# Two transformer blocks on one core: projections ahead of the block boundary, parts loaded into 48 partitions, and expert results scattered to token order

## The reference

```
xn = layernorm(x)
s  = attention(xn)          # block 0: linear attention, 16 heads of 16; block 1: causal softmax attention with ALiBi, 16 heads of 16
g  = mixture(xn)            # router, the 2 best of E experts per token, plus one shared expert
x  = x + s * silu(g)

mixture: y = shared_mlp(xn) + sum over the 2 chosen experts of share_r * expert_r(xn)
         expert(x) = (silu(x Wg) * (x Wu)) Wd,  inner size 176;  E = 8 in block 0, 16 in block 1
         share = the two best router values, divided by their sum
```

## Time and profile before

| | |
|---|---|
| time, median of 3 runs | 731.95 us (731.43 to 732.06) |
| profiled execution: its own time, its span | 733.88 us, 732.1 us |
| mean granted TensorE clock | 0.937 |
| experts 0 | 134.1 to 225 us |
| shared 0 | 225 to 340.4 us |
| first scores of sequence 0 | 374.0 us |
| first transposed scores (attention proper) | 394.4 us |
| experts 1 | 587.3 to 669.9 us |
| shared 1, chunks 1 to 3 | 669.9 to 709.3 us |
| end of the span | 732.1 us |

### The profile page before, as it was taken

How to read it: one execution, slowest core, us unless ns; L and a number is a source line. 1 busy time by engine, 2 the same in 40 slices (tenths; PEclk the granted TensorE clock), 3 DMA queues, 4 the chain that set the end, 5 groups by cost and what they waited for, 6 DMA issues and landing times.

```text
span 732.1 us, 12664 instructions
## 1 busy us (share of the span) xinstructions
PE 612.6 (84%) x4090; PEld 483.0 (66%) x4090; DVE 410.4 (56%) x992; ACT 331.3 (45%) x715; POOL 158.1 (22%) x172
## 2 busy tenths in 40 slices
PE   2989993699999998999558899998988789999750
PEld 2958882599998887886344565666665468886430
DVE  6176664255544365656726756645543456665468
ACT  2223331366555444444513435444445468886331
POOL 0127533000004440401301013221122100002662
PEclk9999997699999999999859989999999989999985
DMA  9903553343322950201693854767922035542334
GB/s 323 310 29 125 146 161 130 91 130 116 117 83 83 277 114 8 59 0 41 133 127 100 120 111 110 150 97 160 173 60 66 1 96 163 160 153 87 90 101 134
DMA packets 85560, 86.64 MB, mean 118 GB/s; under 512 B 19727, under 2 KB 77026, under 8 KB 85218
## 3 DMA queue, kind: packets, MB, share of 16 engines
q1 hardware_dynamic: 78842, 68.92, 38.1%
q0 software_dynamic: 6144, 16.79, 7.8%
q10 hardware_dynamic: 512, 0.13, 0.1%
HBM read 51.40 MB, written 34.28 MB: 117 GB/s over the span
## 4 chain that ended last, share of the span: by engine, by line
PE 39%; DVE 8%; ACT 4%; DMA 2%; issue 2%; SPq 1%; POOL 0%; ACTq 0%; DVEq 0%
PE bank L821 5%; PE bank L885 4%; PE bank L909 3%; PE bank L1019 3%; PE bank L1045 3%; PE bank L972 3%; PE bank L1063 2%; PE bank L873 2%; PE bank L668 2%; PE bank L1021 2%; PE bank L1047 2%; PE bank L839 2%; PE bank L896 1%; DVE mneg L1915 1%; DMA KS<-projection_parts 1%
## 5 line engine op out<-in xcount | busy, mean ns | idle before, releaser
L589 POOL DMA_INDIRECT slots<-xn,slot_of x64 | 66.6, 1041 | 167.7 <-DMA slots<-xn,slot_of 100.4
L1915 DVE TENSOR_REDUCE mneg<-bank 128x2 f32<-128x512 f32 (+1 forms) x96 | 62.7, 685 | 51.0 <-PE bank L1021 50.4
L1752 DVE TENSOR_TENSOR xgl<-bank,xgh 128x256 f16<-128x256 f32 (+1 forms) x86 | 36.4, 424 | 51.9 <-ACT xgh L1310 51.9
L602 POOL DMA_INDIRECT rets<-results,slot_of x32 | 33.4, 1042 | 139.3 <-DMA results<-ys 97.6
L1726 DVE TENSOR_TENSOR hf<-bank,sg 128x512 f32<-128x512 f32 x36 | 24.7, 690 | 61.5 <-PE bank L821 56.8
L1019 PE MATMUL bank<-KS,QS 99*128 99x256 bf16 (+1 forms) x256 | 38.7, 261 | 20.4 <-DMA KS<-projection_parts 11.8
L602 POOL DMA_INDIRECT gu<-results,slot_of x32 | 31.4, 982 | 112.2 <-DMA results<-ys 96.5
L873 PE MATMUL bank<-cf,xn 128*128 128x128 f32 x172 | 36.3, 295 | 19.5 <-DMA xn<-slots 17.1
L1420 ACT ACTIVATE exps_first_keys<-bank 128x512 f32<-128x512 f32 x64 | 34.8, 597 | 29.4 <-PE bank L1047 29.4
L1285 ACT ACTIVATE sg<-bank 128x512 f32<-128x512 f32 x36 | 21.3, 599 | 56.1 <-PE bank L821 56.1
L1759 DVE TENSOR_TENSOR hs<-bank,gs 128x176 f32<-128x176 f32 x86 | 29.3, 341 | 28.9 <-ACT gs L1316 24.4
(11 more groups left out here) (221 smaller groups left out, 1609.6 us busy)
## 6 DMA issues: line engine op xcount, KB each, us to landing
xn<-slots SPq DMA_DIRECT2D x86, 128.0 KB, 2.2
results<-ys SPq DMA_DIRECT2D x86, 128.0 KB, 1.7
projection_parts<-parts SPq DMA_DIRECT2D x16, 384.0 KB, 2.8
QS<-projection_parts SPq DMA_DIRECT2D x48, 128.0 KB
KS<-projection_parts SPq DMA_DIRECT2D x48, 128.0 KB
slots<-zrow SPq DMA_DIRECT2D x1, 6016.0 KB, 21.9
x<-in_x SPq DMA_DIRECT2D x8, 512.0 KB, 6.0
x<-in_w SPq DMA_DIRECT2D x4, 704.0 KB, 8.2
```

Source lines behind the costliest of these rows:

```text
L589: pool.indirect_dma_start(out=slots_dram, out_offset=bass.IndirectOffsetOnAxis(ap=at, axis=0), in_=xn[:, t, :], in_offset=None).then_inc(s ...
L602: pool.indirect_dma_start(out=rets[L][:, t % RETS, r, :], out_offset=None, in_=results_dram[L], in_offset=bass.IndirectOffsetOnAxis(ap=at, ...
L1752: dve.tensor_tensor(xgl[L][:, j % 2, :], PS[j % 2][:, 0:D], high[:, j % 2, :], ALU.subtract)\
L1915: dve.tensor_reduce(mneg[:, qt, h0:h0 + heads], PS[6 + p % 2][:].rearrange("p (n k) -> p n k", n=heads), AX.X, ALU.max, negate=True).then_ ...
```

## The change

1. Six projections (j = 0 to 5) move into `shared(0)`, behind items 15 to 18, 21 and 22, all through PSUM bank 7, with their high and mid parts on ACT, rests on DVE and low parts on POOL. They share one `rest` buffer. The parts of chunk 0 are stored, and sequence 0 is loaded when 22 of 24 down products are done.
2. The DRAM layout of the parts has a fourth copy, so that three parts of a query or key lie side by side. A sequence is loaded by 4 DMAs of 48 partitions instead of 12 of 16. The heads take another order in memory (`column(h)`).
3. The 20 stores of slope and position rows move behind `expert_rows(0)` on SP's queue.
4. A new `first_scores` on PE interleaves sequence 0's scores with the front and router of chunks 2 and 3. DVE interleaves its maxima with the last combinations, updates and normalisations. The Exp of block 1's routing and the copy of the shared down weights on ACT come behind `attention(-1)`.
5. Block 1's row scatters wait for every fourth instead of each. Behind them POOL scatters, for each slot, a label of two numbers (8 bytes: the row of the result in token order, and the token's share). A table of labels is filled at the start with rows past the end, for slots without a token, and read back before experts 1 (`slot_labels`).
6. In experts 1, ACT multiplies each result tile by the share as it copies it (Identity with a scale), and POOL scatters it from `ys` straight to `results_by_token` (47 indirect DMAs) instead of SP's store. SP loads the results of one chunk with two direct DMAs of 512 KB, POOL adds the two experts of each token, and DVE adds the sum. The gather and DVE's `combine` of block 1 go.
7. `shared(1)` for chunks 1 to 3 is one run of nine items on ACT and DVE too, with the additions, silus and updates between the items; the x copies of chunk 2 move into experts 1, and PE's first shared gates stand before the wait for the last result.

```diff
-EARLY_BANK = (0, 1, 2, 3, 1, 2)
+EARLY_BANK = 7
+EARLY = {15: 0, 16: 1, 17: 2, 18: 3, 21: 4, 22: 5}
...
-    parts_dram = nc.dram_tensor("projection_parts", (NCH, 2, 3, 2, 2, P, SEQ), BF16, kind="Internal").ap()
+    parts_dram = nc.dram_tensor("projection_parts", (NCH, 2, 4, 2, HD, H, SEQ), BF16, kind="Internal").ap()
...
+    labels_dram = nc.dram_tensor("slot_labels", (SLOTS[1] * P, 2), F32, kind="Internal").ap()
+    returned_dram = nc.dram_tensor("results_by_token", (2 * NTOK * P + SLOTS[1] * P, D), F32, kind="Internal").ap()
...
+            sp.wait_ge(tokens_set, 2)
+            sp.dma_start(labels_dram.rearrange("(j p) c -> p j c", p=P), unused_labels).then_inc(labels_cleared, 16)
...
             expert_rows(0)
+            sp.wait_ge(rows_set, 3)
+            for h in range(H):
+                sp.dma_start(position_rows_dram[:, h, :], position_row[SLOPE_ROW:ALL_ROWS, :]).then_inc(rows_stored, 16)
+            for n in range(SEQ // 64):
+                sp.dma_start(slope_rows_dram[:, :, 64 * n:64 * n + 64], slope_row[SLOPE_ROW:MAX_ROW]).then_inc(rows_stored, 16)
...
+            def store_parts(i, kind):
+                sp.wait_ge(part_low, after(4 * i + kind + 3))
+                for copies, which in ((slice(kind ^ 1, 3 + (kind ^ 1)), slice(0, 3)),
+                                      (slice(3 * kind, 3 * kind + 1), slice(2 * kind, 2 * kind + 1))):
+                    sp.dma_start(parts_dram[i, kind, copies].rearrange("t b d (h a) n -> (d h) t b (a n)", a=2),
+                                 parts[:, kind, which].rearrange("p t b a n -> p t b (a n)"))\
+                      .then_inc(part_stored[kind], 16)
...
-                for kind, (dst, order) in enumerate(((QS, Q_PART), (KS, K_PART))):
-                    for place, part in enumerate(order):
-                        sp.dma_start(dst[slot][HD * place:HD * place + HD].rearrange("d (a h) n -> d a (h n)", a=2),
-                                     parts_dram[i, kind, part, b].rearrange("a (d h) n -> d a (h n)", d=HD))\
+                for kind, dst in enumerate((QS, KS)):
+                    for u in range(2):
+                        first = 1 - u if kind else u
+                        sp.dma_start(dst[slot][3 * HD * u:3 * HD * (u + 1)].rearrange("p h n -> p (h n)"),
+                                     parts_dram[i, kind, first:first + 3, b].rearrange("t d h n -> d t (h n)"))\
...
+            store_parts(0, 0)
+            store_parts(0, 1)
+            sp.wait_ge(s_down, SHARED[0] * NCH - 2)
+            load_rows(0)
+            load_sequence(0)
...
+            sp.wait_ge(labels_sent, 16 * 2 * NTOK)
+            sp.dma_start(slot_labels, labels_dram.rearrange("(j p) c -> p j c", p=P)).then_inc(labels_landed, 16)
             expert_rows(1)
+            for n in range(YRING):
+                sp.wait_ge(returned[n], 16 * len(range(n, SLOTS[1], YRING)))
+            for c in range(NCH):
+                if c >= 2:
+                    sp.wait_ge(combined, NTOK + 2 * (c - 1))
+                for r in range(2):
+                    row = r * NTOK * P + c * CH
+                    sp.dma_start(rets[1][:, TPC * (c % 2):TPC * (c % 2) + TPC, r, :],
+                                 returned_dram[row:row + CH, :].rearrange("(t p) d -> p t d", p=P))\
+                      .then_inc(back_landed[c % 2], 16)
...
+            low_parts(range(6))
...
+            scatter(1, 4)
+            pool.wait_ge(scattered[1], 16 * 2 * NTOK)
+            pool.wait_ge(ex_set, once(1, 1))
+            pool.iota(own_labels[:, :, 0], [[P, 2 * NTOK]], base=0, channel_multiplier=1,
+                      allow_small_or_imprecise_dtypes=True).then_inc(tokens_set, 1)
+            pool.wait_ge(tokens_set, 3)
+            pool.wait_ge(shares_set, 1)
+            pool.wait_ge(labels_cleared, 16)
+            for n in range(2 * NTOK):
+                if n and n % 8 == 0:
+                    pool.wait_ge(labels_sent, 16 * n)
+                pool.indirect_dma_start(out=labels_dram,
+                                        out_offset=bass.IndirectOffsetOnAxis(ap=slot_of[:, n:n + 1], axis=0),
+                                        in_=own_labels[:, n, :], in_offset=None).then_inc(labels_sent, 16)
...
+            pool.wait_ge(returns_set, 1)
+            for j in range(SLOTS[1]):
+                pool.wait_ge(ey_sb, tile(1, j + 1))
+                pool.indirect_dma_start(out=returned_dram,
+                                        out_offset=bass.IndirectOffsetOnAxis(ap=returns_to[:, j:j + 1], axis=0),
+                                        in_=ys1[:, j % YRING, :], in_offset=None).then_inc(returned[j % YRING], 16)
+            for n in range(NTOK // 2):
+                c, at = n // 2, 2 * n % RETS
+                pool.wait_ge(back_landed[c % 2], 32 * (c // 2 + 1))
+                pool.tensor_tensor(rets1[:, at:at + 2, 0, :], rets1[:, at:at + 2, 0, :], rets1[:, at:at + 2, 1, :], ALU.add)\
+                    .then_inc(pair_summed, 1)
...
+            def next_front(k):
+
+                c, n = k // SHARED[0] - 2, k % SHARED[0]
+                j = EARLY.get(k)
+                if j is not None:
+                    if j == 0:
+                        pe.wait_ge(s_a1, 16 * (4 + HD))
+                        pe.wait_ge(columns_set, 16)
+                    pe.wait_ge(xt_sb, half(1, 2 * (j // 4) + 2))
+                    pe.wait_ge(part_rest, after(j))
+                    project(j, EARLY_BANK)
...
+            def first_scores():
+
+                scores(0, 0)
+                scores(0, 1)
+                value_bias()
+                front(1, NCH - 2)
+                for p in (2, 3, 4):
+                    scores(0, p)
+                router(1, NCH - 2)
+                for p in range(5, 11):
+                    scores(0, p)
+                front(1, NCH - 1)
+                scores(0, 11)
+                max_transposes(0)
+                pe.wait_ge(vbias_ready, 1)
+                pe.wait_ge(s_sb[1], after(0))
+                values(0)
+                pe.wait_ge(lg_read, NCH - 1)
+                router(1, NCH - 1)
+                j = projected(-1)
+                pe.wait_ge(v_sb, after(1))
+                project(j, PROJECT_BANK[0])
+                project(j + 1, PROJECT_BANK[1])
...
+            pe.wait_ge(eh_set, tile(1, SLOTS[1]))
+            shared_gates(1, SHARED[1])
             pe.wait_ge(ey_sb, tile(1, SLOTS[1]))
-            shared(1, (1, 2, 3), nothing)
+            shared(1, (1, 2, 3), nothing, begun=True)
...
+                        if j >= YRING:
+                            act.wait_ge(returned[j % YRING], 16 * (j // YRING))
+                        act.activation(ys1[:, j % YRING, :], PS[6 + j % 2][:, 0:D], ACT.Identity,
+                                       scale=slot_labels[:, j, 1:2]).then_inc(ey_sb, 1)
...
+            def rest_part(j, bank):
+
+                bias = 2 * (j % 2) + j % 4 // 2
+                dve.wait_ge(part_high, after(j + 1))
+                dve.wait_ge(part_low, after(j if j < 6 else j - 1))
+                dve.scalar_tensor_tensor(out=by_sequence(rest_of(j)), in0=by_sequence(PS[bank][:]),
+                                         scalar=c1_heads[:, bias:bias + 1], in1=part_of(j, 0),
+                                         op0=ALU.add, op1=ALU.subtract).then_inc(part_rest, 1)
...
+            def add_returned(n):
+
+                at = 2 * n % RETS
+                dve.wait_ge(s_res, half(1, n + 1))
+                dve.wait_ge(pair_summed, n + 1)
+                dve.tensor_tensor(xn[:, 2 * n:2 * n + 2, :], xn[:, 2 * n:2 * n + 2, :], rets1[:, at:at + 2, 0, :],
+                                  ALU.add).then_inc(combined, 1)
...
+            sums(1, NCH - 2, front1)
+            combine(NTOK - 4)
+            combine(NTOK - 3)
+            maxima(0, 0)
+            normalise(1, NCH - 2, front1)
+            maxima(0, 1)
+            maxima(0, 2)
+            combine(NTOK - 2)
+            combine(NTOK - 1)
+            maxima(0, 3)
+            update_x(0, 2 * NCH - 2)
+            maxima(0, 4)
+            update_x(0, 2 * NCH - 1)
+            maxima(0, 5)
+            sums(1, NCH - 1, front1)
+            maxima(0, 6)
+            maxima(0, 7)
+            read_logits(NCH - 2)
+            normalise(1, NCH - 1, front1)
+            for p in (8, 9, 10):
+                maxima(0, p)
+            dve.wait_ge(vbias_ps, 1)
+            vbias = r1[:]
+            dve.tensor_tensor(vbias, vbias, PS[TAIL_BANK][:, 0:D], ALU.add).then_inc(vbias_ready, 1)
+            maxima(0, 11)
+            read_max(0)
+            read_logits(NCH - 1)
+            j = projected(-1)
+            rest_part(j, PROJECT_BANK[0])
+            rest_part(j + 1, PROJECT_BANK[1])
...
+                if k == 5:
+                    add_returned(0)
+                    add_returned(1)
+                if k == 6:
+                    low_x(1, 3)
+                    update_x(1, 0)
+                if k == 7:
```

(27 more changed lines are left out.)

376 lines of the change are left out of this document (177 added, 199 removed).

## The result

The changed kernel takes 725.14 us (median of 7 runs, 722.00 to 727.87) beside 732.05 us for the kernel before on the same chip (728.99 to 734.50). The ratio is 0.9906, 95% interval 0.9878 to 0.9935: 0.9% faster, some 7 us, where 32 were forecast and 712 was the high end of the range. The profiled execution took 725.74 us, its span is 724.0.

What follows compares the result with a forecast made beforehand. PE is busy 84% of the span, so gains lie in its waits at the block boundary and tail: -15.9 + 2 + 0.5 - 18.8 = -32.2, from 731.95 to 699.8 us; range 687 to 712.

Steps and rivals of the forecast that it cites:

- Start of experts 0: Block 0's first expert tile: slot loads go at 121.1 instead of 131.8, PE starts at 130.4 for 134.09, -3.7 us.
- Six early projections: In shared 0: 1.76 us of PE each, +10.5 us; ACT and DVE parts lie beside it, one item's slack covers rests.
- Load of sequence 0: Block boundary: 1.57 MB at 211 GB/s takes 7.5 us (4.3 to 12.8), scores start at 352.0 instead of 374.0.
- First scores: From scores to first transposed scores: 26.5 us (20.4 to 31) for 20.4, attention starts at 378.5, -15.9 in all.
- Behind it: Start of attention: ACT's routing Exp and shared-weight copy now stand ahead of the first exponentials, +2 us (0 to 3).
- Attention: Stage between first scores and experts 1: left nearly as it is.
- rival 1 and 2: Experts 1: result scatters become the bound, 743.8, 5%; or labels come late and delay slot row loads, 725.4, 7%.
- rival 4: Half the tail or boundary gain is given back, by late returns or slow first scores and rests: 708 to 718, 14%.
- Labels and results by token: Label DMAs cost nothing; result scatters hidden in experts 1; x copies less early shared gates cost +0.5 us.
- rival 3: First label DMA is slow, so ACT stands 16 us for weight piece 0 at 100 ns a packet: 715.8, 8%.
- rival 1: Result scatters become the bound of experts 1: +44 us at 2.7 us each, 743.8, 5%.
- Tail: Behind experts 1: 43.4 us for 62.2, -18.8, including 4.5 (0 to 6.8) for POOL's sums slowing DVE.

Runs made afterwards that it cites:

- split_stores: Changed kernel with the parts of a chunk stored in two halves, the first ahead of the earlier sequence load: 719.89 us, ratio 0.9831.
- loads16: Changed kernel with each 48-partition sequence-load DMA cut into three of 16 partitions: 735.18 us, ratio 1.0072.
- tail_fenced: Kernel before plus results by token alone, with down weights, label load and slot row loads held until row maxima landed: 715.79 us, ratio 0.9787.
- fenced: Changed kernel with stores split in halves, and down weights, label load and slot row loads held until row maxima landed: 716.68 us, ratio 0.9784.
- tail_only: Kernel before with the results-by-token part alone, boundary and sequence loads as before: 722.99 us, ratio 0.9881.

## Why the prediction was too low

**Start of experts 0: right.** 130.82 for a forecast 130.4; the first slot loads were issued at 120.84.

**Six early projections: the direct cost right, the cover wrong.** Six at 1.76 us are 10.5, shared 0 grew by 17.0 (13.7 in `split_stores`, so part of it varies from one execution to the next). The sum had no term for what they do to neighbours: at item 17 PE waits 4.25 us for 2.75, and in the last item 0.82 and 0.98 for 0.23. In the trace ACT's high part and VectorE's rest of a projection stand in the chain of sums and square root that item 17 waits for; no run took them out of it, so that this is the cause is not shown. From 317 to 322 us the granted clock was 0.57.

**Load of sequence 0: right within its range.** Issued at 347.9 (5.9 late, with shared 0), 12.35 us to the scores for a forecast 10.0. The traffic ran at 197 GB/s in the wait, near the 211 taken. By the table of the Trainium skill ("SBUF — State Buffer", section "Door 1: The DMA port swizzle") 16 partitions reach 4 ports and partitions 0 to 47 reach 8, but 48 to 95, which half of these DMAs fill, reach 12; the prediction had 8 for both. By that rule the rate would at least double; 202 GB/s for the 125 of `loads16` is 1.6 times: the direction agrees, not the size.

**First scores: mis-sized.** 31.1 us, the high bound, for 26.5. It was 22.7 to the cast of the maxima, with VectorE busy 17.0 of them (21 were estimated for it) and the granted clock 0.58. The step "the last router and projections follow the last maximum" had left out the values: values, router and projections are 8.6 us of PE behind it (382.8 to 391.4), where the kernel before had the projections alone, 3.6 us, under the maxima's DMA. The clock was not granted sooner.

**Behind it: right.** +2 were forecast; from the first transposed scores to the next cast it is 19.3 us for 17.3, with 1.6 us of PE waiting for ACT's exponentials.

**Attention: the step that failed.** "Attention is left nearly as it is", and the queued transfers beside it were costed only by whether their own users were in time. They were: sequence loads, labels (loaded at 548.4, forecast 543) and slot rows cost their users nothing. What the forecast had not asked is who else is on the DMA engines when they move. The stores in one go make the load of sequence 6 six us late, label scatters slow it further, and it then lies on the maxima of sequence 5: +7.2 us in that round, +2.1 in the next, +0.8 before them, +2.0 the term above, -0.2: the 11.9 of the stage. Of the 9.3 us of those two rounds 6.1 are longer waits from cast to scores; the rest fits the half clock behind them, at most 3.7. With the transfers moved aside (`tail_fenced`) the stage is 193.0. That queues share the engines was in the forecast only as rival 1 and 2, for scatters. Without the 9.9 us of this stage the forecast's misses add up to 14.2 (714 us): that is rival 4 as it was written (first scores of 31 us, shared 0 paying for the rests, 708 to 718), which had been given 14%. Attention put the time past it.

**Labels and results by token: right as to their users.** ACT took weight piece 0 at 55.70, so rival 3 did not occur; experts 1 took 82.8 us with 47 scatters, so rival 1 did not either.

**Tail: right within 1.6 us.** First the pair sums of POOL, then VectorE's additions and its last operation:

```profile
689.36 2.69 POOL L736 TENSOR_TENSOR gu<-gu 128x512 f32<-128x512 f32 x2 [7.75 <-DMA gu<-results_by_token]
```

```profile
690.91 3.37 DVE L1923 TENSOR_TENSOR xn<-xn,gu 128x512 f32<-128x512 f32 x2 [1.23 <-POOL gu L736]
...
701.83 1.75 DVE L1923 TENSOR_TENSOR xn<-xn,gu 128x512 f32<-128x512 f32 x1
...
704.71 0.68 DVE L1923 TENSOR_TENSOR xn<-xn,gu 128x512 f32<-128x512 f32 x1
...
720.40 0.69 DVE L1931 TENSOR_TENSOR x<-x,xn 128x512 f32<-128x512 f32 x1
```

VectorE goes on at +11.9 (forecast +12.5) and needs 33.1 us from there for 30.9. An addition takes 0.68 alone and 1.75 beside POOL's sum (699.85 to 703.0); with the exclusive port lock of the Trainium skill ("SBUF — State Buffer", section "SBUF: two separate sides") the trace agrees. Summed over the operations beside the eight sums the excess is about 6.7 us, the high bound of a term taken at 4.5.

**Why the boundary won nothing.** The wait of 11.75 us and the stores were indeed taken away, and first transposed scores came at 391.4, or 387.6 in `split_stores`, for 394.4. But 10.5 us of PE work moved from a place where it partly filled a wait into a place without one, with 3 to 6 us more of stalls and half clock; first scores take 31.1 us for 20.4, and in them now stands work that VectorE did during the wait; and some 4 us go behind (attention takes 196.8 us in `fenced`, 193.0 in `tail_fenced`). The traces show these places; no run took each of them away by itself, so the shares are argued and not shown.

## What to carry to other kernels

For each transfer that a change moves, enlarges or bunches, list not only who waits for it but which small, urgent DMA is due while it is under way; PE stood up to 10 us for two DMAs of 8 KB behind a 1.57 MB load in another queue, and then worked at half clock. If a bulk load has slack, hold it until the urgent one has landed: two waits in one queue were worth 7 us in one kernel here (`tail_only` to `tail_fenced`) and 3 in another (`split_stores` to `fenced`, at the edge of what these runs can tell). Measure the parts of a compound change apart: here the results by token paid, the moved stores perhaps, and the largest part, the boundary, nothing. When matmuls are put in to keep the clock up, count their own time: they can hold up what they were meant to speed up.

## What the runs showed of the hardware

With scatters of 128 pieces of 8 bytes in flight, up to eight, a bulk load of some 250 GB/s ran at 29 to 74 GB/s for 4 us in `tail_only`, with the engines some 40% busy; thirteen of fourteen kernels with such scatters show the slow start. The Trainium skill ("DMA: Bandwidth & Descriptors", section "Specifications") says that below 512 bytes the DMA engine reads, modifies and writes; no run here shows whether that is the reason. While one queue moved 203 GB/s in rows of 8 KB, the first packet of another queue's DMA came 4.0 us behind its issue (7.7 in `loads16`), for 1.2 otherwise. PE kept at work held its clock at 2.4 GHz over the whole of the first scores (granted 1.00); the stage was 29.9 us for 31.1, with 11.4 us of PE's time in it gone to the fillers.
